# Low halves of the cosine features on GpSimd, those of the sine features on VectorE

## The reference

```python
xb = 2.0 * jnp.pi * xyz[..., None] * freq_bands      # 6 bands
feat = jnp.concatenate([jnp.sin(xb), jnp.cos(xb)], axis=-1)
return jnp.einsum('bnf,of->bno', feat.reshape(b, n, -1), W)
```

## Time and profile before

| what | value |
|---|---|
| median of three runs | 1764.85 us |
| the profiled execution's own time | 1762.65 us |
| its span, first to last instruction | 1760.9 us |
| token stage, first instruction to the first after its barrier | 0 to 312.98 us |
| busy in the span: TensorE, VectorE, ScalarE, GpSimd | 85%, 73%, 60%, 23% |

### The profile page before, as it was taken

How to read it: one execution, slowest core, us unless ns; L and a number is a source line. 1 busy time by engine, 2 the same in 40 slices (tenths; PEclk the granted TensorE clock), 3 DMA queues, 4 the chain that set the end, 5 groups by cost and what they waited for, 6 DMA issues and landing times. The chain is left out here.

```text
span 1760.9 us, 36645 instructions
## 1 busy us (share of the span) xinstructions
PE 1491.3 (85%) x14396; PEld 1120.5 (64%) x14396; DVE 1278.0 (73%) x2547; ACT 1049.8 (60%) x1871; POOL 413.2 (23%) x424
## 2 busy tenths in 40 slices
PE   5899997797588888999999719995697999999795
PEld 5889887697455767644445618994675734446474
DVE  5988897499799547379993758884755489984566
ACT  6998897434588255448995306663003558994565
POOL 0000000101665210469900117871002210000200
PEclk9999999699599989979997659997887979997897
DMA  5110100100000100035500732221100000000101
GB/s 145 28 41 28 37 1 26 29 1 1 8 2 2 35 1 14 2 106 166 162 2 1 207 122 57 66 63 55 38 1 14 1 1 2 2 2 1 35 1 37
DMA packets 52748, 67.96 MB, mean 39 GB/s; under 512 B 11535, under 2 KB 41489, under 8 KB 52578
## 3 DMA queue, kind: packets, MB, share of 16 engines
q1 hardware_dynamic: 46022, 50.30, 9.5%
q0 software_dynamic: 3840, 9.18, 1.8%
q10 hardware_dynamic: 2716, 6.14, 1.4%
HBM read 46.97 MB, written 18.65 MB: 37 GB/s over the span
## 5 line engine op out<-in xcount | busy, mean ns | idle before, releaser
L2066 DVE TENSOR_REDUCE att_max<-banks 104x1 f32<-104x512 f32 (+1 forms) x480 | 296.6, 684 | 13.0 <-PE banks L1980 9.1
L2101 ACT ACTIVATE att_p<-banks 104x514 f32<-104x514 f32 (+1 forms) x480 | 262.8, 599 | 39.0 <-PE banks L2025 28.4
L339 PE MATMUL banks<-tok_wT,feature_halves 128*128 128x192 f16 x2592 | 228.8, 249 | 23.0 <-DVE feature_halves L365 11.9
L339 PEld LDWEIGHTS banks<-tok_wT,feature_halves 128*128 128x128 f16 x2592 | 216.6, 99 | 32.1 <-DVE feature_halves L365 17.7
L2041 PE MATMUL banks<-att_p,att_v 104*32 104x257 f32 (+1 forms) x1920 | 165.8, 419 | 0.6
L2025 PE MATMUL banks<-att_q,att_kT 64*104 64x257 f16 (+1 forms) x960 | 157.7, 310 | 2.6 <-ACT att_p L2101 2.5
L2025 PEld LDWEIGHTS banks<-att_q,att_kT 64*104 64x104 f16 (+1 forms) x960 | 62.4, 126 | 109.5 <-ACT att_p L2101 83.0
L1980 PE MATMUL banks<-att_kT,att_q 64*104 64x512 f16 (+1 forms) x480 | 126.3, 426 | 5.9 <-DVE att_max L2066 3.5
L365 DVE TENSOR_TENSOR feature_halves<-features,feature_halves 128x2048 f16<-128x2048 f32 x54 | 123.4, 2286 | 5.7 <-ACT feature_halves L462 5.7
L134 PE MATMUL banks<-ones 128*128 128x256 f16 x654 | 86.4, 289 | 27.7 <-PEq L251 13.6
L462 ACT CAST feature_halves<-features 128x2048 f16<-128x2048 f32 x54 | 102.2, 1893 | 10.2 <-PE banks L339 9.4
(11 more groups left out here) (472 smaller groups left out, 3429.2 us busy)
## 6 DMA issues: line engine op xcount, KB each, us to landing
expert_w_in<-in_L_ffn_w_dram SPq DMA_DIRECT2D x16, 576.0 KB, 4.6
expert_w_halves<-expert_w_halves SPq DMA_DIRECT2D x32, 288.0 KB, 2.5
tok_w<-in_L_tok_W_dram ACTq DMA_DIRECT2D x4, 1152.0 KB, 7.2
expert_w2s<-expert_w_halves SPq DMA_DIRECT2D x1, 4608.0 KB
expert_y<-expert_out SPq DMA_DIRECT2D x6, 513.0 KB
expert_w1s<-expert_w_halves SPq DMA_DIRECT2D x2, 1536.0 KB
raw<-in_x_dram SPq DMA_DIRECT2D x2, 1152.0 KB, 5.4
expert_w1s<-expert_w_halves SPq DMA_DIRECT2D x3, 768.0 KB
```

What stands on the lines that cost most here:

```text
L339: ins = pe.matmul(c.bank[t // 2][:, (t % 2) * D:(t % 2 + 1) * D], fh[:, s, q, z, t * 128:(t + 1) * 128], wT[:, y, k, 6 * q + wf, :], start ...
L2066: dve.reduce_max(mx[0:qn, n // NS % 2, 2 * gi + e, k:k + 1], bank_of(unit)[0:qn, 0:KEYS], X).then_inc(maxed, 1)
L2101: act.activation(p[0:kn, n % 4, :, :], c.pair[2 + n % 2][0:kn, :].rearrange("p (e q) -> p e q", e=2)[:, :, 0:HALF], ACT.Exp, scale=scale). ...
```

## The change

`low_part` on VectorE is cut to the sines (128 x 1024), and GpSimd gets a loop that makes the low part of the cosines (128 x 1024) in every step. It has a semaphore of its own, `flow_p`; TensorE (before the low matmuls) and ScalarE (before it overwrites the features' buffer) now wait for both.

```diff
+        flow_p = c.sem("features_low_pool")
...
                     for z, y in ((0, 0), (0, 1), (1, 0)):
                         if z:
                             pe.wait_ge(flow, n + 1)
+                            pe.wait_ge(flow_p, n + 1)
...
                     dve.wait_ge(fhigh, n + 1)
-                    dve.tensor_tensor(fh[:, s, :, 1, :], feat[:, s, :, :], fh[:, s, :, 0, :], ALU.subtract
+                    dve.tensor_tensor(fh[:, s, 0, 1, :], feat[:, s, 0, :], fh[:, s, 0, 0, :], ALU.subtract
                                       ).then_inc(flow, 1)
...
                     if n >= 2:
                         act.wait_ge(flow, n - 1)
+                        act.wait_ge(flow_p, n - 1)
...
                 pool.memset(c.ones[:, :], 1.0).then_inc(set_, 1)
+                for n in range(N):
+                    s = n % 2
+                    pool.wait_ge(fhigh, n + 1)
+                    if n >= 2:
+                        pool.wait_ge(fused, n - 1)
+                    pool.tensor_tensor(fh[:, s, 1, 1, :], feat[:, s, 1, :], fh[:, s, 1, 0, :], ALU.subtract
+                                       ).then_inc(flow_p, 1)
+                    pool.wait_ge(flow_p, n + 1)
```

## The result

| | kernel before | changed kernel |
|---|---|---|
| median of eight runs each | 1758.99 us | 1780.64 us |
| all runs | 1749.09 to 1766.78 | 1773.73 to 1789.68 |
| profiled execution's span | 1760.9 us | 1775.3 us |
| first instruction of VectorE after the stage's barrier | 313.02 us | 332.79 us |

The changed kernel is slower: ratio 1.0138, 95% interval 1.0106 to 1.0171. The forecast was 1785 us against a median of 1764.85, a ratio of 1.0114, and a range of 1772 to 1802. With five more executions the median of the kernel before is 1758.99 us, so the forecast's 20 us stand against 21.65.

The account below looks back on a forecast made before the run. ScalarE was taken to bound the second half at about 4.38 us a step, and in the first to wait for VectorE's low part. 18.2 + 1.5 + 0 = +19.7 us, so 1764.85 + 20 = 1785 us; range 1772 to 1802.

Parts of the forecast that it names:

- GpSimd's subtraction of 1024 columns, alone: GpSimd's new low part of the cosines, at 1.91 ns a column: 2.13 us for 1024 columns.
- VectorE's half of the low part: VectorE's low part with 1024 columns fewer: 1.07 us less per step, so 1.21 us.
- a settled pair of steps, second half: VectorE's 6.65 us per two steps plus twice 1.92 us taken by GpSimd through the shared SBUF port: 10.49 us.
- steps 33 to 53: Second half of the stage: 5.25 us a step instead of 4.34, 20 steps 0.91 us longer each, +18.2 us.
- steps 25 to 33: Around the middle: the pause of about 4 us stays, other steps go from 5.07 to 5.25 us, +1.5 us.
- steps 0 to 25: First half: 0, since 5.25 us a step is below the 5.58 of now; bounds -7.0 to +7 us.
- rival C: Chain closes on top of the port: gaps of about 0.5 us a step over 46 steps, +43 us, 1808; chance 0.10.
- The gain of 7.0 us: First half: ScalarE's 8 waits for VectorE's low part, 7.0 us, all that a shorter low part can give back directly.
- The latency of GpSimd's part: GpSimd's low part is done 2.2 us after the cast, TensorE asks some 2.8 us after it: hidden, taken by itself.
- Rival A: No collision that counts: second half stays at 4.38 us a step, first loses 7.0 us of waiting, 1758 us; chance 0.08.
- Rival B: Only two-operand instructions collide: 8.5 us of shared time per two steps, nothing measurable changes, 1764 us; chance 0.06.
- What would show it: Profile signs: casts 5.2 to 5.3 us apart, VectorE durations spread, ScalarE below 17 of 20 us, GpSimd's subtraction 2.1 to 3.5.

Follow-up runs that it names:

- experiment 5: The changed kernel run a second time, unaltered: 1782.56 us as the median of seven executions, ratio 1.0118; next stage at 334.05 us.
- the third experiment: Kernel before, with the cosines' low part left out, VectorE making only the sines' and GpSimd idle: 1747.49 us, ratio 0.9942; next stage at 306.10 us.
- experiment 1: Kernel before, plus 54 GpSimd subtractions of 128 x 1024 in unused memory, for which no engine waits: next stage at 371.56 us, 58.5 later.
- experiment 2: Kernel before, plus a GpSimd memset of 2400 float16 columns per step, which reads nothing: next stage at 330.91 us.
- experiment 4: Changed kernel with GpSimd's low part in one half of the stage only: next stage at 319.74 us (first half, +6.7) and 332.10 us (second half, +19.1).

## Why the prediction was right, and where it was not

The sum came out at +19.7 us, and the stage ends 19.8 us later. The direction, the mechanism and the price of one instruction were right; that the sum agrees to 0.1 us is luck. Its terms did not come out as well, and the errors cancel; besides, a second execution of the same kernel has 1.3 us more (experiment 5):

| term | forecast | measured |
|---|---|---|
| GpSimd's subtraction of 1024 columns, alone | 2.13 us | 2.13 us (the shortest; 2.53 at the median) |
| VectorE's half of the low part | 1.21 us | 1.22 us |
| a settled pair of steps, second half | 10.49 us | 10.42 us |
| steps 33 to 53 | +18.2 us | 100.39 - 86.71 = +13.7 us |
| steps 25 to 33 | +1.5 us | 44.53 - 44.71 = -0.2 us |
| steps 0 to 25 | 0, -7 to +7 | 144.61 - 139.42 = +5.2 us |
| behind the cast of step 53 | 0 | 20.90 - 19.82 = +1.1 us |

- *Second half: mechanism and price right, the count of steps too high.* The pattern of 10.4 us a pair sets in only some five steps after step 33, and the last pair is faster again. The forecast multiplied the settled period by all 20 steps. The casts were said to come 5.2 to 5.3 us apart; they do in the settled pairs (5.21), but the mean from step 33 to 53 is 5.02.
- *Around the middle: the collision is there and costs nothing.* VectorE's rests come at the slow pace on both sides of the pause, 10.41 us for two steps from 167.14 and again from 221.39 us:

```profile
167.14 1.27 DVE L356 SCALAR_TENSOR_TENSOR angle_rest<-raw_T,freq,turns 128x1024 f32<-128x1024 f32 x1
...
177.55 1.27 DVE L356 SCALAR_TENSOR_TENSOR angle_rest<-raw_T,freq,turns 128x1024 f32<-128x1024 f32 x1
...
215.50 2.29 DVE L356 SCALAR_TENSOR_TENSOR angle_rest<-raw_T,freq,turns 128x1024 f32<-128x1024 f32 x1 [0.79 <-ACT features L458]
...
221.39 1.27 DVE L356 SCALAR_TENSOR_TENSOR angle_rest<-raw_T,freq,turns 128x1024 f32<-128x1024 f32 x1
...
231.80 1.28 DVE L356 SCALAR_TENSOR_TENSOR angle_rest<-raw_T,freq,turns 128x1024 f32<-128x1024 f32 x1
```

But from step 25 to step 36 the intervals between casts are those of the kernel before, the pause excepted (9.72 us for the pair behind step 25). By the timeline VectorE is ahead of ScalarE there, uses the lead up, and gets it back in the pause; at 215.50 us it is so far ahead that it waits 0.79 us for ScalarE to be done with a buffer. The casts slow down only when this lead is used up. The forecast compared mean paces, 5.07 us a step against 5.25, and had no term for the lead. No run took the lead away to test this.
- *First half: the bound from the port is not the bound.* I took 0 because 5.25 us a step lie below 5.58. The measured step is 5.78, and there are three steps of 8.4 us in the first 25, where there was none over 7.1, much as rival C has it. One of them in the timeline of the changed kernel:

```profile
77.48 0.48 ACT L424 ACTIVATE tok_wT<-banks 128x384 f16<-128x384 f32 x1
77.70 2.17 POOL L487 TENSOR_TENSOR feature_halves<-features,feature_halves 128x1024 f16<-128x1024 f32 x1 [2.16 <-ACT feature_halves L465]
77.81 3.14 DVE L367 TENSOR_TENSOR feature_halves<-features,feature_halves 128x1024 f16<-128x1024 f32 x1
...
81.01 2.18 PE L341 MATMUL banks<-tok_wT,feature_halves 128*128 128x192 f16 x16 [3.05 <-DVE feature_halves L367]
81.03 1.06 ACT L457 ACTIVATE features<-angle_rest 128x1024 f32<-128x1024 f32 x1 [3.07 <-issue]
```

GpSimd takes the lock 0.11 us ahead of VectorE's low part, which belongs to the step before and for which both TensorE and ScalarE wait: 3.05 and 3.07 us of idle time. For ScalarE's wait the profile names no releaser ("issue"); that it is the low part follows from the program, and from all seven such waits, each of which ends less than 0.1 us behind the end of a low part. Between 22 and 167 us ScalarE's waits are, in us in total, times, longest:

```profile
ACT features L457 <- issue: 11.7, 7, 3.1
ACT feature_halves L465 <- PE banks L341: 5.5, 8, 1.6
```

In the kernel before they were 7.0 and 4.9 us. The 4.7 and 0.6 us more are, to 0.1 us, the 5.2 us that the first half got longer. So the lower granted clock there, which could delay a cast only through the matmuls it waits for, explains at most the 0.6 us. C was priced at 0.5 us a step everywhere; it cost 0.2 us a step, in the first half. The 7.0 us of waits that a shorter low part can save did not go: the longer waits came in their place.
- *The gain of 7.0 us* that shorter low parts could give back is real where GpSimd does nothing: 7.5 us at step 25 and 6.9 at the next stage in the third experiment.
- *The latency of GpSimd's part is hidden*, as forecast: in the changed kernel's profile no engine's idle time ends with GpSimd's subtraction, and experiment 1 costs more than the change itself although no step waits for it.
- *Rival A* (no collision) is ruled out by the durations of four VectorE groups. *Rival B* (only two-operand instructions) fails too: the turns went from 0.75 to 2.63 us beside GpSimd's subtraction, and in experiment 2 it is the other way round than B has it.
- *What would show it*: the spread of lines 356, 361, 242 and 367, and line 375 unmoved at 0.55 us came as said; ScalarE, at 17.00 of 20 us, is on the edge of the "below 17"; GpSimd's rows lie between 2.13 and 3.24 us, as 2.1 to 3.5 was said.
- *A slip beside the sum.* The estimate of 2.25 us for the subtraction was said to make the sum about 5 us larger. It is 0.12 us more than 2.13, so for the 28 steps in which the sum counts it, it is 3.4 us.

## What to carry to other kernels

An idle GpSimd is no free place for elementwise work as long as VectorE works from SBUF to SBUF: its time is added to VectorE's, and 1024 columns cost 1.9 us there to save 1.07. Before work is moved between the two, look in the trace for a VectorE instruction that takes longer beside a GpSimd one, and ask whether the operands come from SBUF or PSUM. A mean pace is not enough for a forecast: a chain can wait for one badly placed instruction where the mean has slack, and an engine that is ahead can hide a collision for some steps. And count what the third engine allows: with ScalarE at 19.94 of 20 us, the whole second half had nothing to give even to a free helper.

## What the runs showed of the hardware that was not expected

- A GpSimd memset of 2.10 us holds VectorE's fast one-operand instructions to its end, but leaves two-operand ones untouched (1277 ns for 1279, the mean of 54 rests), although it costs the stage 17.9 us through the first kind alone.
- When the rows of the two engines begin within 0.02 to 0.03 us of each other, either can go first; in one program at the same place of the pattern both happened (experiment 4), and when VectorE lost, its low part took 3.17 instead of 1.21 us. Such ties are one reason why the costs of two halves of a change do not add up (6.7 + 19.1 for 19.8 us); the pause in the middle, 9.0 or 10.3 us in two executions of one kernel, is another.
- VectorE's low part of the weights, from PSUM, kept 0.55 us in all runs (549 to 556 ns on average), also with GpSimd's subtraction running beside it over its whole length.
